# Quantizing the down weights earlier, and reordering the first and last stages, in a one-core kernel of attention by autocorrelation with an FP4 feed-forward

## The reference

```python
def attention(Q, K, V):                 # Q = layernorm(x), K = V = context
    q, k, v = (Z @ Wq + bq).T           # 256 -> 16 columns
    corr = real(ifft(fft(q) * conj(fft(k)))).mean(axis=(0, 1))
    W, I = top_k(corr, 12); W = softmax(W)
    R = sum(w * roll(v, -shift) for w, shift in (W, I))
    return broadcast(R, 16 heads) @ Wout + bout
x = x + attention(layernorm(x), ctx, ctx)
def fp4_quant_dequant(x):               # blocks of 16 in the last dim
    scale = max(max(abs(xb)) / 6, 1e-12)
    return GRID[searchsorted(MID, abs(xb / scale))] * sign(xb) * scale
def ffn(x):                             # gate, up: 704 x 256; down: 256 x 704
    h = silu(fp4_linear(x, w_gate)) * fp4_linear(x, w_up)
    return fp4_linear(h, w_down)        # both operands quantized
x = x + ffn(layernorm(x))
```

## Time and profile before

| what | value |
|---|---|
| median of 3 runs | 526.64 us (526.01 to 527.78) |
| profiled execution, its own time | 528.21 us |
| its span, first to last instruction | 526.4 us |
| TensorE matmul busy | 476.7 us (91%) |
| VectorE busy | 456.9 us (87%) |
| ScalarE busy | 391.9 us (74%) |
| GpSimd busy | 254.2 us (48%) |
| mean granted TensorE clock | 0.964 |

### The profile page before, as it was taken

One profiled execution on the slowest core, in us unless ns is written; L12 is line 12 of the kernel. 1 busy time (PEld: TensorE's weight loads), 2 busy tenths in 40 slices (PEclk: granted clock), 3 DMA queues, 4 the chain that ended last, 5 costly groups with the idle time before them and its releaser, 6 DMA issues.

```text
span 526.4 us, 10114 instructions
## 1 busy us (share of the span) xinstructions
PE 476.7 (91%) x3490; PEld 315.4 (60%) x3490; DVE 456.9 (87%) x762; ACT 391.9 (74%) x670; POOL 254.2 (48%) x326
## 2 busy tenths in 40 slices
PE   4599897858699999999999999999999999899957
PEld 4587787723355666666656666666666666466635
DVE  3789967598679999999999999999999999999981
ACT  3267875775978888888888788888888877766661
POOL 3225550256245566665655556666565558333330
PEclk9989997978899999999999999999999999899989
DMA  8988810432055676576675575656666564444636
GB/s 274 346 264 269 277 51 26 86 85 56 1 95 106 134 131 129 120 132 128 143 125 116 121 140 122 130 116 126 141 121 138 117 118 93 97 97 95 133 69 150
DMA packets 164723, 68.68 MB, mean 130 GB/s; under 512 B 129088, under 2 KB 164416, under 8 KB 164672
## 3 DMA queue, kind: packets, MB, share of 16 engines
q1 hardware_dynamic: 164672, 68.03, 57.3%
HBM read 27.38 MB, written 9.18 MB: 69 GB/s over the span
## 4 chain that ended last, share of the span: by engine, by line
issue 34%; POOL 21%; DVE 20%; PE 13%; ACT 5%; DMA 4%; SPq 1%; POOLq 1%; DVEq 1%; ACTq 0%
POOL ctx_sb L466 13%; POOL sl L482 6%; DVE w_q_lo L1144 4%; DVE ctx_sb L1097 3%; DVE y_h L1176 2%; DVE x_t L895 2%; PE ps L724 2%; ACT h_c L536 2%; PE ps L842 2%; ACT h_c L533 2%; PE ps L843 1%; DMA w_raw<-in_L_ffn_w_up_dram 1%; PE ps L704 1%; PE ps L844 1%; PE ps L714 1%
## 5 line engine op out<-in xcount | busy, mean ns | idle before, releaser
L842 PE MATMUL ps<-guT_hi,a_xT 128*128 128x512 f16 (+1 forms) x384 | 141.9, 370 | 14.1 <-DVE hb L1092 7.4
L843 PE MATMUL ps<-guT_lo,a_xT 128*128 128x512 f16 (+1 forms) x384 | 142.1, 370 | 0.0
L844 PE MATMUL ps<-guT_hi,a_xT 128*128 128x512 f16 (+1 forms) x384 | 141.6, 369 | 0.0
L852 PE MATMUL ps<-dT_hi,hqT 128*128 128x256 f16 x704 | 130.5, 274 | 7.6 <-ACT a_xT L594 5.7
L466 POOL TENSOR_TENSOR ctx_sb<-w_q_lo,sl 128x704 f16<-128x704 f16 x62 | 96.2, 1574 | 29.4 <-DVE ctx_sb L1097 29.3
L533 ACT ACTIVATE h_c<-y_h 128x1408 bf16<-128x1408 bf16 (+3 forms) x39 | 47.8, 1226 | 75.9 <-DVE y_h L1176 58.7
L854 PE MATMUL ps<-dT_lo,hqT 128*128 128x256 f16 x384 | 88.4, 275 | 0.0
L517 POOL TENSOR_TENSOR xs<-xs,w_raw 128x512 f32<-128x512 f32 x30 | 36.0, 1200 | 101.1 <-issue 101.1
L852 PEld LDWEIGHTS ps<-dT_hi,hqT 128*128 128x128 f16 x704 | 69.3, 98 | 18.7 <-issue 6.0
L842 PEld LDWEIGHTS ps<-guT_hi,a_xT 128*128 128x128 f16 x384 | 38.1, 99 | 62.5 <-issue 15.7
L844 PEld LDWEIGHTS ps<-guT_hi,a_xT 128*128 128x128 f16 x384 | 38.2, 100 | 40.5 <-issue 3.5
(11 more groups left out here) (161 smaller groups left out, 863.9 us busy)
## 6 DMA issues: line engine op xcount, KB each, us to landing
xs<-in_x_dram SPq DMA_DIRECT2D x16, 512.0 KB, 6.1
ctx_sb<-in_ctx_dram SPq DMA_DIRECT2D x16, 512.0 KB, 5.1
out_dram<-a_xT SPq DMA_DIRECT2D x64, 128.0 KB, 2.0
w_raw<-a_scratch SPq DMA_DIRECT2D x60, 128.5 KB, 2.7
hqT<-ctx_sb SPq DMA_TRANSPOSE x64, 3.8
w_raw<-in_L_ffn_w_down_dram SPq DMA_DIRECT2D x1, 704.0 KB, 6.3
w_raw<-in_L_ffn_w_gate_dram SPq DMA_DIRECT2D x1, 640.0 KB, 5.9
w_raw<-in_L_ffn_w_up_dram SPq DMA_DIRECT2D x1, 640.0 KB, 6.9
```

What stands on the lines that cost most here:

```text
L842: pe.matmul(dst, xt[:, c, :], guT[0][:, c, n0:n1], start=(c == 0), stop=False)
L843: pe.matmul(dst, xt[:, c, :], guT[1][:, c, n0:n1], start=False, stop=False)
L844: last = pe.matmul(dst, xt[:, KC + c, :], guT[0][:, c, n0:n1], start=False, stop=(c == KC - 1))
L852: pe.matmul(dst, hqT[:, j % 4, c, :], dT_hi[:, c, :], start=(c == 0), stop=False)
```

## The change

It moves these things:

- The down weights' load goes ahead of the last two loads of x and context. `w_prepare(1)` runs in the first phase's iteration 14; `w_largest(1)`, `w_scales(1)` and the two `w_segment` right after its end; both `w_finish` in the second DRAM trip instead of stages -1 and 0. ScalarE's `w_split` of these come ahead of the first weight copies, all eight gate and up copies come after the exponential (`EARLY` goes from 5 to 4), then `w_hi`; GpSimd's `w_lo` of them follow its `pick`.
- Down fills 8 and 9 go ahead of the constant matmuls, whose number goes from 20 to 28; fill 10 goes to the end of TensorE's stage 0, fill 11 between the two tiles of stage 1, fill 12 to its end. ScalarE's copies are spread over stages -2 to 1, and in stage 0 its `silu(0)` comes first.
- GpSimd's `w_lo` of gate and up comes one iteration later and waits for VectorE's product of the next segment. `low_h` waits for `scaling_h` of the stage before (`yh_done`).
- VectorE's x work of pair 2 is interleaved in stage 1 instead of leading it. `low_h` of pairs 29 and 30 is VectorE's. In stages 31 and 32 the order is new on VectorE, ScalarE and SyncE; the last pair's y has a buffer of its own (`z_y`).

```diff
@@ -273,7 +274,7 @@
-        EARLY, GU_FILLS = 5, 2 * 2 * KC
+        EARLY, GU_FILLS = 4, 2 * 2 * KC
@@ -327,10 +328,11 @@
             for i in range(2, NQ):
+                if i == NQ - 2:
+                    down_v = w_raw[:, 256 * GU_CH:WCOLS].rearrange("p (c n) -> p c n", n=FF)
+                    sp.dma_start(down_v, w_down.rearrange("(c p) n -> p c n", p=P)).then_inc(s["d_loaded"], 16)
                 load_x(i)
                 load_c(i)
-            down_v = w_raw[:, 256 * GU_CH:WCOLS].rearrange("p (c n) -> p c n", n=FF)
-            sp.dma_start(down_v, w_down.rearrange("(c p) n -> p c n", p=P)).then_inc(s["d_loaded"], 16)
             sp.dma_start(bout_bc[:, 0:D], bout.rearrange("(a n) -> a n", a=1).broadcast_to([P, D])
@@ -360,7 +362,10 @@
                 else:
-                    sp.wait_ge(s["loh"], i + 1)
+                    if i // 2 >= NP - 3:
+                        sp.wait_ge(s["z_lo"], i // 2 - NP + 4)
+                    else:
+                        sp.wait_ge(s["loh"], i + 1)
                     sp.wait_ge(s["h4_steps"], K_HQ * (i // 2 + 1))
@@ -388,14 +393,15 @@
                     turn_h(2 * st - 5)
+                if tile_ok(2 * st - 8):
+                    store(2 * st - 8)
                 if st == NP + 1:
+                    store(2 * st - 7)
                     turn_h(2 * NP - 2)
                     turn_h(2 * NP - 1)
-                if tile_ok(2 * st - 8):
-                    store(2 * st - 8)
                 if pair_ok(st + 1):
                     turn_x(st + 1)
-                if tile_ok(2 * st - 7):
+                if tile_ok(2 * st - 7) and st != NP + 1:
                     store(2 * st - 7)
@@ -420,6 +426,8 @@
                 pool.wait_ge(s["w_hi"], g + 1)
+                if g + 1 < N_GU:
+                    pool.wait_ge(s["w_steps"], finish_at(g + 1) + 3)
                 pool.tensor_tensor(chunks_of(w_q[1], g), runs_of(g), chunks_of(w_q[0], g), ALU.subtract
@@ -438,8 +446,8 @@
                     rstd_a(i + 2)
-                if turn(i - 2) is not None:
-                    w_lo(turn(i - 2))
+                if turn(i - 3) is not None:
+                    w_lo(turn(i - 3))
@@ -447,11 +455,13 @@
                                channel_multiplier=1).then_inc(s["pick_set"], 1)
+            w_lo(N_GU)
+            w_lo(N_GU + 1)
...
                 pool.wait_ge(s["z_sh"], t + 1)
-                pool.wait_ge(s["loh"], 2 * (NP - 2))
+                pool.wait_ge(s["z_lo"], 1)
                 cols, two = slice(t * RUN_H, (t + 1) * RUN_H), "p (b two) -> p b two"
@@ -486,7 +496,8 @@
                     low_scales(NP - 1)
-                if pair_ok(st - 3) and st <= NP + 1:
+                if pair_ok(st - 3) and st < NP:
+                    pool.wait_ge(s["yh_done"], st - 1)
                     low_h(st - 3)
@@ -517,8 +528,6 @@
                                        ).then_inc(s["x1_done"], 1)
-                if st in (0, 1):
-                    w_lo(N_GU + st)
@@ -576,12 +585,13 @@
             keep_v(NQ // QT - 1)
-            evacuate_weights(act, range(EARLY))
+            w_split(N_GU)
+            w_split(N_GU + 1)
             act.wait_ge(s["t_steps"], 3)
             act.activation(wexp[:, :], corr[:, 0, 0:P], ACT.Exp, bias=nmx[:, 0:1]).then_inc(s["t_exp"], 1)
-            evacuate_weights(act, range(EARLY, GU_FILLS))
-            w_split(N_GU)
-            w_split(N_GU + 1)
+            evacuate_weights(act, range(GU_FILLS))
+            w_hi(N_GU)
+            w_hi(N_GU + 1)
             act.preload_act_table(ACT.Silu)
@@ -600,7 +610,7 @@
                 act.wait_ge(s["z_y"], t + 1)
-                top = tile_of(high_half(y_h[:, :]).bitcast(BF16), t)
+                top = tile_of(high_half(z_y).bitcast(BF16), t)
                 c, tt = tile_of(z_c, t), tile_of(z_t, t)
@@ -654,39 +664,43 @@
                 j, n = st - 1, st + 2
-                if st in (0, 1):
-                    w_hi(N_GU + st)
-                if st <= 0:
-                    if st < 0:
-                        scale_high(st)
-                        split_x(n)
+                if st < 0:
+                    scale_high(st)
+                    split_x(n)
                     normalise_x(st + 3)
                     square_x(st + 4)
-                    if st == 0:
-                        scale_high(st)
-                        split_x(n)
-                        silu(0)
-                        silu(1)
+                    if st >= -2:
+                        evacuate_weights(act, range(GU_FILLS + 2 + st, GU_FILLS + 3 + st))
+                elif st == 0:
+                    silu(0)
+                    normalise_x(st + 3)
+                    square_x(st + 4)
+                    scale_high(st)
+                    silu(1)
+                    split_x(n)
+                    evacuate_weights(act, range(GU_FILLS + 2, GU_FILLS + 3))
                 elif st < NP:
...
                     silu(2 * st)
-                    if st == 2:
-                        evacuate_weights(act, range(GU_FILLS + 2, len(FILLS)))
+                    if st == 1:
+                        evacuate_weights(act, range(GU_FILLS + 3, GU_FILLS + 4))
                     normalise_x(st + 3)
...
                     silu(2 * st + 1)
-                    if st == 1:
-                        evacuate_weights(act, range(GU_FILLS, GU_FILLS + 2))
                     split_h(j)
                     split_x(n)
+                    if st == 1:
+                        evacuate_weights(act, range(GU_FILLS + 4, len(FILLS)))
                 elif st == NP:
+                    residual(2 * st - 8)
+                    residual(2 * st - 7)
                     last_split(0)
-                    residual(2 * st - 8)
+                    residual(2 * st - 6)
+                    residual(2 * st - 5)
                     last_split(1)
-                    residual(2 * st - 7)
-                else:
+                elif st > NP + 1:
                     residuals(2 * st - 8)
@@ -766,6 +780,7 @@
             correlate(NQ - 2)
+            spread_largest(1, bank(4)[:, 3 * P:4 * P])
             correlate(NQ - 1)
@@ -802,8 +817,7 @@
-            pe.wait_ge(s["qk_ev"], NQ)
-            spread_largest(1, bank(5)[:, 0:P])
+            pe.wait_ge(s["w_pool"], 2)
             pe.wait_ge(s["g_io"], 32)
@@ -856,9 +870,13 @@
             pe.wait_ge(s["w_ev"], GU_FILLS)
+            pe.wait_ge(s["x1_done"], 2)
+            pe.wait_ge(s["w_lo"], len(SEGS))
+            for f in range(GU_FILLS, GU_FILLS + 2):
+                transpose_weights(f)
             pe.wait_ge(s["id_out"], 1)
-            for _ in range(20):
-                pe.matmul(bank(6)[:, 0:P], ones[:, :], ident[:, :], start=True, stop=True)
+            for _ in range(28):
+                pe.matmul(bank(4)[:, 0:P], ones[:, :], ident[:, :], start=True, stop=True)
             def gate_and_up(i):
@@ -871,14 +889,11 @@
                     gate_and_up(2 * n)
-                    if n == 2:
-                        for f in range(GU_FILLS + 2, len(FILLS)):
-                            transpose_weights(f)
+                    if n == 1:
+                        transpose_weights(GU_FILLS + 3)
                     gate_and_up(2 * n + 1)
-                if n == 1:
-                    pe.wait_ge(s["w_lo"], len(SEGS))
-                    for f in range(GU_FILLS, GU_FILLS + 2):
-                        transpose_weights(f)
+                if n < 2:
+                    transpose_weights(GU_FILLS + 2 + 2 * n)
                 if n == 3:
@@ -1010,7 +1025,13 @@
                     w_segment(turn(i))
+                if i == NQ - 2:
+                    w_prepare(1)
             evac_qk(NQ - 1)
+            w_largest(1, bank(4)[:, 3 * P:4 * P])
+            w_scales(1)
+            w_segment(N_GU)
+            w_segment(N_GU + 1)
             cs = s["c_steps"]
@@ -1023,9 +1044,6 @@
             dve.tensor_scalar(tiny[:, 0:RUN_H], tiny[:, 0:RUN_H], TINY_FLOOR * X_SCALE, None, ALU.max)
-            w_prepare(1)
-            w_largest(1, bank(5)[:, 0:P])
-
             dve.wait_ge(s["late_loaded"], 32)
@@ -1055,15 +1073,9 @@
             dve.reciprocal(tsum[:, 1:2], tsum[:, 0:1]).then_inc(ts, 1)
-            w_scales(1)
-            w_segment(N_GU)
-            w_segment(N_GU + 1)
-            dve.tensor_scalar(inv_out[:, :], w_inv[:, 1:2], h_tmp[:, 1:2], None, ALU.mult).then_inc(cs, 1)
-            dve.wait_ge(cs, 5)
-            dve.reciprocal(out_fac[:, :], inv_out[:, :]).then_inc(cs, 1)
-            dve.wait_ge(cs, 6)
-            dve.wait_ge(s["trx"], 2 * NQ)
-            dve.tensor_scalar(ident_out[:, :], ident[:, :], out_fac[:, 0:1], None, ALU.mult).then_inc(s["id_out"], 1)
+            dve.wait_ge(s["trc"], 2 * NQ)
+            w_finish(N_GU)
+            w_finish(N_GU + 1)
             for h in range(2):
@@ -1079,6 +1091,13 @@
+            dve.tensor_scalar(inv_out[:, :], w_inv[:, 1:2], h_tmp[:, 1:2], None, ALU.mult).then_inc(cs, 1)
```

(41 more changed lines are left out.)

## The result

The changed kernel takes 504.22 us (median of 4 runs, 503.61 to 505.49) against 527.21 us for the kernel before (526.01 to 527.96): ratio 0.957, 95% interval 0.954 to 0.960, 23.0 us less. The forecast was 504.5. The profiled execution took 504.39 us with a span of 502.6 us (before 526.4).

The account below looks back on a forecast made before the run. It took the loop as VectorE's own work plus GpSimd's tail, TensorE close behind. Terms -1.7 + 1.3 - 11.0 - 11.0 = -22.4 took the profiled 528.2 to 505.8, median 504.2, put at 504.5 us; range 500 to 508.

Parts of the forecast that it names:

- First phase: Image groups before attention: later `w_lo` frees four segment products, about half of 3.4 us comes through; -1.7 us (0 to -3.4).
- Attention phase: Before the stages: ScalarE's copies and TensorE's last transposes come late, the constants end after the weights land; +1.3 us (+0.4 to +2.4).
- Opening: Stages 1 to 3: work moved out and fills placed earlier shorten them by 4.1, 4.5 and 2.4; -11.0 us (-4.1 to -12).
- the first step: Stage 1: both `w_finish` leave stages -1 and 0, it starts near 117, stage 2 at 126.3 instead of 130.38; -4.1 us.
- Stage 2's step: Stage 2: without two down copies ahead of `split_h(0)` and the 5.24 us fill wait, 11.4 instead of 15.90; -4.5 us.
- Settled loop: Settled stages: VectorE's order is unchanged and the `yh_done` wait hides behind the `yx_done` wait; cost 0, period 11.93 us.
- End: From stage 27: TensorE's earlier start gives 4.8 us, unblocked last products and down products 6.2; -11.0 us (-4.8 to -12).
- 1: Rival on the opening: clock falls, constants and ScalarE's chain run long, only stage 1's 4.1 us come; 512 us, chance 0.10.
- 2: Rival on the end: only TensorE's 4.8 us come, last DMA transposes queue behind SyncE's stores; 510.5 us, chance 0.08.
- 4: Rival: nothing changes, the new waits are covered and the moved work was hidden; 526.6 us, chance 0.02 with small gains.
- 3: Rival, stages 27 to 29: GpSimd wins the ports at `scaling_x`, VectorE stands 1.5 us each, up to 4.5; 509, chance 0.05.
- 5: Rival, slower: TensorE's lag at stage 4 passes 3.7 us and each settled stage grows; 530.5 at 1.1 each, chance 0.04.

Follow-up runs that it names:

- experiment 1: Kernel before with only the gate and up `w_lo` one image group later, waiting for the next segment's product; 0.9966 of the kernel before, -1.8 us.
- Experiment 9: Changed kernel without the eight constant pairs ahead of the product with cT; 0.955 of the kernel before, -1.0 us against the changed kernel.
- experiment 7: Changed kernel with x work ahead of `gate_up` in stage 1 and the x split ahead of the silus in stage 0 again; +6.7 us against it.
- experiment 5: Changed kernel with all five down fills and their copies back in their old places; 0.969 of the kernel before, +6.6 us against the changed kernel.
- experiment 6: Changed kernel without the 28 constant products ahead of pair 0; 0.962 of the kernel before, +2.7 us against the changed kernel.
- experiment 11: Changed kernel with GpSimd's low scales made in their own stage; 501.87 us, 0.952 of the kernel before, -2.7 us against the changed kernel.
- experiment 3: Changed kernel without the wait for `yh_done` in `low_h`; 0.967 of the kernel before, +5.3 us against the changed kernel.
- experiment 8: Changed kernel with 13 extra constant products on TensorE ahead of down(0) in stage 3; 0.956 of the kernel before, -0.3 us against the changed kernel.

## Why the prediction was right

The sum was -22.4 for the profiled execution and -23.8 came; the medians differ by 23.0, where the forecast had 22.1. Part of this agreement is luck: 1.6 of the 23.8 us are the early data and the part ahead of the fourth `kT`, which differ in the same way between two kernels with the same first phase, and errors in the terms below cancel. The terms, in the order of the prediction:

**First phase, -1.7: right in mechanism, too large in size.** The products went from 1.53 to 0.69 us as forecast, but the traces give 1.1 us for it (experiment 1): about a third of the 3.4 came through, not half. The trace after shows -2.6 because 1.6 us came from elsewhere. The `w_prepare` fitted its wait.

**Attention phase, +1.3: right** (+1.30; the eight traces with the new order and eight pairs take 19.87 to 20.41 us, the three with the old one 18.69 to 19.44), and for the reason given: the transposes come late and the constants behind them run to 92.3. Experiment 9 adds that the constants can't simply go: without them the product ran at half the clock.

**Opening, -11.0: right in size (-11.2), the first step's reason not enough.** Its parts were forecast as -4.1, -4.5 and -2.4 and came as -4.1, -4.8 and -2.4. The step "VectorE's two `w_finish` (5 us) leave stages -1 and 0. Stage 1 then starts near 117" is not what the first edit does by itself: with `w_finish` out and the old order stage 1 starts 22.4 us after the second `s_nm` and not 17.6 (experiment 7). The order of x and h is needed for it; whether `w_finish` had to go too was not tested. Stage 2's step names the two copies ahead of `split_h(0)`; experiment 5 gives them 1.9 of the 4.8 us. The other 2.9 (13.00 there, 15.90 before) go with the tiles of pair 1: before, `silu(3)` ran at 131.48, 1.1 us behind the stage's start, in experiment 5 at 125.95, 1.7 ahead of it. Experiment 7 gives the order of x and h 1.0 us of stage 2 (12.15 for 11.11), with `silu(3)` only 0.05 us ahead of the stage's start; the rest was not taken apart. Stage 3's 2.4 us are the third fill's wait for a bank (2.8 in experiment 5). The clock that the prediction took as kept was, and its price came as its bound said (1.8 us at stage 1, experiment 6).

**Settled loop, 0: right** (11.93 in all kernels that keep the old low scales). The -0.3 is one stage of 12.2 us, of which before had two and after has one. The reading "VectorE's own work plus GpSimd's tail" was right too, and experiment 11 bears it out: without GpSimd's tail the period falls.

**End, -11.0: right (-10.9), its two terms mis-sized.** -4.8 for the wait and -6.2 for the order were forecast; the wait is worth 5.9 to 6.9 and the order 4.0 to 5.0. TensorE's earlier end was well forecast (-5.1). What was put down wholly to the order was partly the wait's: with TensorE last, y is ready for the split of h. The stages 28 to 30 took 10.79, 10.19 and 9.77 us: VectorE and not TensorE still paced their starts, while TensorE, always busy, fell back from 1.1 us behind it (stage 27) to 5.5 (stage 31) and set only the end.

**Rivals.** 1, 2 and 4 are refuted by the traces (2's own sum comes to 510.4, not 510.5). 3 is too: at `scaling_x` in stages 27 to 29, the last that have one, VectorE starts first, and GpSimd 0.16 us later. The Trainium skill, "SBUF — State Buffer", section "SBUF: two separate sides", says that the engine that starts first keeps the shared ports. The trace agrees, with 0.69 us for VectorE and 3.38 for GpSimd there, and with 1.74 for VectorE in experiment 3, where GpSimd is first. 5 is refuted by experiment 8, at a lag (6.2 us) beyond its own point of 3.7.

## What to carry to other kernels

Before charging moved work to the path, look whether the engine waited where the work was: in the old order 5 us of VectorE in the opening were free, and bringing that order back, of two small groups of instructions, cost more than 5 us. Where a slow engine shares ports with a fast one, release its long instructions so that they start just after the fast engine's last short product has started: that was worth 6 to 7 us here, in stages 27 to 30. A wait of 0.64 us in a loop whose engine looks like the bound is worth removing, but the gain ends at the next engine's sum (11.65 us for TensorE), and here the last stages gave part of it back.
